# Reciprocals in another step, first keys from float32 rows, half of the first query copies on GpSimd, and the last expert added and stored by 128 tokens

## What is computed

```python
Q, K, V = (heads(x @ W.T + b) for each of q, k, v)      # x is layer-normed first
scores = einsum('bhld,bhrd->bhlr', Q, K) / sqrt(8)
scores = scores + einsum('bhld,lrd->bhlr', Q, rel_k)    # rel_k by clipped distance
attn = softmax(scores)
out = einsum('bhlr,bhrd->bhld', attn, V) + einsum('bhlr,lrd->bhld', attn, rel_v)
x = x + out @ Wo.T + bo
...
# feed-forward: 2 shared experts, 8 routed ones with the best two chosen per token
y = einsum('enh,ehd->end', gelu(einsum('nd,edh->enh', xf, w1) + b1), w2) + b2
x = x + shared_out + einsum('ne,end->nd', comb, y)
```

## Time and profile before

| | |
|---|---|
| median of 3 runs | 2062.05 us (2060.28 to 2062.34) |
| profiled execution: its own time | 2061.96 us |
| profiled execution: span on the chip | 2060.2 us |
| PE busy | 2018.7 us, 98% |
| DVE, ACT, POOL busy | 78%, 73%, 59% |
| granted TensorE clock, mean | 0.995 |

### The profile page before, as it was taken

The page is one execution under the profiler, slowest core; times in us unless marked ns, Lnnn a source line. Parts: engine busy times, 40 slices in busy tenths (PEclk is TensorE's granted clock), DMA queues, the critical chain, the costliest instruction groups (busy, mean ns, idle before and its releaser), DMA issues.

```text
span 2060.2 us, 86849 instructions
## 1 busy us (share of the span) xinstructions
PE 2018.7 (98%) x37410; PEld 1497.1 (73%) x37410; DVE 1606.0 (78%) x3739; ACT 1509.4 (73%) x3341; POOL 1216.6 (59%) x1285
## 2 busy tenths in 40 slices
PE   4999999999999999999999999999999999999999
PEld 3777777777777777777777777777777777777776
DVE  6877897788778877887897788778877777676765
ACT  4767677777677766667667767667666888888887
POOL 4554465456445645554455446445443889988897
PEclk8999999999999999999999999999999999999999
DMA  4212311321231122112211321223122221222120
GB/s 112 74 47 69 83 46 48 83 66 49 57 82 57 47 69 73 55 46 69 77 53 46 84 67 46 57 73 68 46 54 50 27 32 27 28 27 33 24 31 12
DMA packets 256658, 113.05 MB, mean 55 GB/s; under 512 B 143018, under 2 KB 253492, under 8 KB 256276
## 3 DMA queue, kind: packets, MB, share of 16 engines
q1 hardware_dynamic: 255796, 107.10, 21.5%
q10 hardware_dynamic: 480, 0.39, 0.1%
HBM read 83.34 MB, written 8.39 MB: 45 GB/s over the span
## 4 chain that ended last, share of the span: by engine, by line
PE 90%; DVE 5%; ACT 2%; POOL 1%; issue 1%; DMA 0%; SPq 0%; ACTq 0%; DVEq 0%; POOLq 0%
PE ps L1592 21%; PE ps L1527 12%; PE ps L1612 10%; PE ps L1534 9%; PE ps L1622 8%; PE ps L1545 7%; PE ps L1810 3%; PE ps L1812 3%; PE ps L1811 3%; PE ps L1792 3%; PE ps L1794 3%; PE ps L1793 3%; ACT probs L793 1%; DVE keys L1270 1%; PE ps L1501 1%
## 5 line engine op out<-in xcount | busy, mean ns | idle before, releaser
L793 ACT ACTIVATE probs<-ps,neg_max 128x512 f32<-128x512 f32 x1024 | 690.5, 686 | 345.4 <-DVE neg_max L1030 345.3
L1030 DVE TENSOR_REDUCE neg_max<-ps 128x1 f32<-128x512 f32 x1024 | 635.3, 682 | 148.3 <-PE ps L1534 144.3
L557 POOL TENSOR_TENSOR stat_hi<-q_twice,mask8h 128x1024 f16<-128x1024 f16 x128 | 242.5, 1895 | 533.9 <-PE ps L1534 487.9
L1592 PE MATMUL ps<-const,probs 128*128 128x128 f32 x4096 | 500.6, 275 | 4.1 <-issue 1.6
L1592 PEld LDWEIGHTS ps<-const,probs 128*128 128x128 f32 x4096 | 450.2, 141 | 36.1 <-issue 20.3
L1035 DVE COPY probs_t<-ps 128x512 f32<-128x512 f32 x512 | 340.4, 685 | 109.1 <-PE ps L1592 103.7
L783 ACT ACTIVATE probs_t<-ps 128x512 f32<-128x512 f32 x512 | 280.0, 595 | 121.1 <-PE ps L1592 117.1
L690 POOL TENSOR_TENSOR probs_t<-probs,probs_t 128x1024 f16<-128x1024 f32 x160 | 341.4, 2157 | 30.6 <-ACT probs_t L875 29.9
L1527 PE MATMUL ps<-keys,stat_hi 128*32 128x512 f16 x4096 | 318.1, 383 | 0.0
L1534 PE MATMUL ps<-rk_split,stat_rel 96*32 96x512 f16 (+2 forms) x4096 | 281.7, 340 | 0.0
L573 POOL TENSOR_TENSOR stat_rel<-q_rel,mask4h 96x1024 f16<-96x1024 f16 x128 | 251.3, 1963 | 46.2 <-PE ps L1534 30.5
(11 more groups left out here) (192 smaller groups left out, 2861.4 us busy)
## 6 DMA issues: line engine op xcount, KB each, us to landing
rv_step<-in_rv_win SPq DMA_DIRECT2D x128, 512.0 KB, 3.8
keys<-keys SPq DMA_DIRECT2D x56, 96.0 KB, 2.9
x_pair<-in_x SPq DMA_DIRECT2D x8, 512.0 KB, 4.6
rel_scratch<-rel_t SPq DMA_DIRECT2D x256, 16.0 KB, 2.9
x_pair<-in_x SPq DMA_DIRECT2D x16, 256.0 KB, 3.2
x_pair<-rel_scratch SPq DMA_DIRECT2D x64, 64.0 KB, 4.1
out<-keys SPq DMA_DIRECT2D x16, 256.0 KB, 2.3
q_twice<-q_hi SPq DMA_DIRECT2D x28, 128.0 KB, 2.4
```

The lines of the kernel that those rows point to most:

```text
L793: nc.scalar.activation(probs[:, q, :], ps[:, i, :], ACT.Exp, bias=neg_max[:, q:q + 1], accum_out=row_sum[parity][:, s * QUADS + q:s * QUAD ...
L1030: nc.vector.tensor_reduce(neg_max[:, q:q + 1], ps[:, i, :], op=ALU.max, axis=AX_X, negate=True).then_inc(max_done, 1)
L1592: last = nc.tensor.transpose(ps[:, bank, rt * P:(rt + 1) * P], probs[:, q, rt * P:(rt + 1) * P], ident)
```

## The change

It has four parts.

1. The reciprocals of a pair move from round (0, 1) of the next pair to round (7, 1), in the last pair to (4, 1).
2. The first keys: ACT makes a float32 copy `first_wk` of the key weights times the scale, and two float32 copies `first_xn` of the transposed rows out of PSUM. PE projects the first keys with one float32 matmul for each sequence instead of three float16 ones. ACT's copy `first_k` is gone: `k_hi` and `k_lo` are made straight from PSUM.
3. Of the first queries' four copies, the two that stay in their own partitions are made by POOL, as 64x256 float16 copies; SP issues the other two and the two of the low parts. The later columns are still copied by SP alone.
4. The last expert of the last batch writes its four parts of 128 tokens to four banks, with a semaphore for each; DVE adds each part when it is done, and SP stores each with its own DMA.

```diff
+def last_bank(t):
+    return (0, 1, 7, up_bank(EXPERTS - 2, 0))[t]
...
-        first_k = attn_t[:, TOK:2 * TOK].rearrange("p (b c) -> p b c", b=2)
+        first_xn = attn_t[:, TOK:2 * TOK]
...
-                    for copy in range(2):
+                    for copy in range(2) if both else (1 - half,):
                         sp.dma_start(part(q_twice[64 * copy:64 * copy + 64, half, :]), part(q_hi[64 * half:64 * half + 64, :])).then_inc(landed, 16)
...
-            store(B - 1, 1)
-            sp.wait_ge(stored, START + 16 * B)
+            for t in range(TPB):
+                sp.wait_ge(last_ready, t + 1)
+                sp.dma_start(out[(B - 1) * L + t * P:(B - 1) * L + (t + 1) * P, :], acc[:, 1, t, :]).then_inc(last_stored, 16)
+            sp.wait_ge(stored, START + 16 * (B - 1))
+            sp.wait_ge(last_stored, 16 * TPB)
...
             pool.wait_ge(setup_dve, SETUP_FIRST)
+            pool.wait_ge(hi_ready, START + 2)
+            for half in range(2):
+                rows = slice(64 * half, 64 * half + 64)
+                nc.gpsimd.tensor_copy(q_twice[rows, half, :].rearrange("p (b c) -> p b c", b=2)[:, :, 0:P],
+                                      q_hi[rows, :].rearrange("p (b c) -> p b c", b=2)[:, :, 0:P]).then_inc(first_high, 1)
+            pool.wait_ge(first_high, 2)
             for b in range(2):
                 split_low(0, b)
...
-            def first_plain_keys(b, bank):
+            def first_high_keys(b, bank):
                 act.wait_ge(proj_done, START + 2 + b + 1)
-                nc.scalar.activation(first_k[:, b, :], ps[:, bank, :], ACT.Copy, scale=1.0 / W_SCALE).then_inc(k_ready, 1)
-
-            def first_high_keys(b):
-                act.wait_ge(k_ready, START + b + 1)
-                nc.scalar.activation(k_hi[0][:, b, FAR_COLS:KEYS], first_k[:, b, :], ACT.Identity, bias=bks_col[:, 0:1])
-                nc.scalar.activation(k_hi[0][:, b, 0:FAR_COLS], first_k[:, b, FAR * P:L], ACT.Identity, bias=bk_far_col[:, 0:1]).then_inc(hi_ready, 1)
+                nc.scalar.activation(k_hi[0][:, b, FAR_COLS:KEYS], ps[:, bank, :], ACT.Identity, bias=bks_col[:, 0:1]).then_inc(k_ready, 1)
+                nc.scalar.activation(k_hi[0][:, b, 0:FAR_COLS], ps[:, bank, FAR * P:L], ACT.Identity, bias=bk_far_col[:, 0:1]).then_inc(hi_ready, 1)
...
+            nc.scalar.activation(first_wk[:], w_qkv_s[:, 1, :], ACT.Copy, scale=SCALE).then_inc(first_rows, 1)
...
+            for half in range(2):
+                act.wait_ge(xn_low, START + half + 1)
+                nc.scalar.activation(first_xn[:, half * L:(half + 1) * L], ps[:, half, :], ACT.Copy).then_inc(first_rows, 1)
...
-                nc.vector.scalar_tensor_tensor(k_lo[:, b, FAR_COLS:KEYS], first_k[:, b, :], bks_col[:, 0:1], k_hi[0][:, b, FAR_COLS:KEYS], ALU.add, ALU.subtract)
+                nc.vector.scalar_tensor_tensor(k_lo[:, b, FAR_COLS:KEYS], ps[:, bank, :], bks_col[:, 0:1], k_hi[0][:, b, FAR_COLS:KEYS], ALU.add, ALU.subtract)
...
-                if (s, j) == (0, 1) and not first:
+                if (s, j) == (7 if ahead else 4, 1) and not first:
                     reciprocals(pair - 1, 1 - parity)
...
+            def last_expert(b, slot):
+                e = EXPERTS - 1
+                for t in range(TPB):
+                    dve.wait_ge(last_down, t + 1)
+                    nc.vector.scalar_tensor_tensor(acc[:, slot, t, :], ps[:, last_bank(t), 0:D],
+                                                   comb[:, slot, t, e:e + 1], acc[:, slot, t, :], ALU.mult, ALU.add).then_inc(last_ready, 1)
...
             for b in range(2):
-                project_keys(0, b, 2 + b)
+                pe.wait_ge(first_rows, b + 2)
+                nc.tensor.matmul(ps[:, 2 + b, :], first_wk[:], first_xn[:, b * L:(b + 1) * L], start=True, stop=True).then_inc(proj_done, 1)
                 natural_queries(0, b, 6 + b)
```

More of the change, by code:

```diff
@@ L375, in store_rel, with first_queries @@
                     sp.dma_start(rel_scratch[bass.ds(row, 32), cols], rel_t[32 * a:32 * a + 32, twos % 2, :]).then_inc(rel_stored[twos % 2], 16)
[L377 removed]
+            def first_queries(cols, landed, both):
                 def part(rows):
@@ L1321, in batch @@
                 for e in range(EXPERTS):
-                    expert(b, slot, e)
+                    if ahead or e < EXPERTS - 1:
+                        expert(b, slot, e)
+                    else:
+                        last_expert(b, slot)
                     if ahead:
@@ L1812, in down @@
                         last = nc.tensor.matmul(y, hid_l[:, place, k, rows], w2_h[:, e, k, :], start=False, stop=k == 1)
-                last.then_inc(down_done, 1)
+                    if final:
+                        last.then_inc(last_down, 1)
+                if not final:
+                    last.then_inc(down_done, 1)
             def batch(b, slot, ahead, after):
@@ L1823, in batch @@
                         prepare_gates(b + 1, 1 - slot, 1)
-                    down(b, slot, e)
+                    down(b, slot, e, not ahead and e == EXPERTS - 1)
                     if ahead:
```

23 lines of the change are left out of this document (12 added, 11 removed).

## The result

| | |
|---|---|
| before | 2061.76 us, median of 4 (2060.28 to 2062.34) |
| the change | 2072.57 us, median of 4 (2072.21 to 2074.78) |
| ratio | 1.0055, 95% interval 1.0043 to 1.0067 |
| profiled execution: its own time, span | 2072.38 us, 2070.6 us |

The changed kernel is 0.55% slower, where 2056.4 us and faster was predicted.

What follows compares the result with a forecast made beforehand. The prediction took PE as the bound, with 90% of the span, so edits count only where PE stands still. It summed 2061.96 - 4.7 + 0.2 + 0.7 - 1.8 + 0 = 2056.4 us, 8-in-10 range 2054.6 to 2059.6.

Steps and rivals of the forecast that it cites:

- What goes at (1, 0): Without the reciprocals, round (1, 0) falls from 6.95 to 6.28 us in pairs 1 to 7: 4.7 us gained.
- What comes in pairs 1 to 6: Reciprocals at (7, 1) mostly fill DVE's idle time and wait briefly for POOL: 0.2 us lost in all, bounds 0 and 2.1.
- My slower rival: At (7, 1) the third DVE instruction meets stat_rel, PE loses 2.3 us in each of six pairs: 2069.9 us, chance 0.06.
- The sign of being wrong: The forecast would be wrong if the reciprocals' instructions at (7, 1) take over 1 us.
- Pair 7: Reciprocals at (4, 1) meet POOL's stat_rel, maxima begin 1.1 us late: 0.7 us lost once, bounds 0.2 and 1.1.
- Start: Keys 0.3, k_lo 0.86, POOL 0.44 and 0.15: PE's first scores come 1.8 us earlier, bounds 0.8 and 2.8.
- the upper bound of my range for the start: At the start, DVE's head_scaled gets in ahead of stat_hi: 2.8 us gained.
- The float32 matmul: First keys on PE: 512 columns take 0.45 us, against 0.64 for three float16 matmuls, done before ACT comes to it.
- End: Tenth expert's additions begin 0.24 us earlier, but four store DMAs issue later: nothing gained, bounds 0.3 either way.
- The sum: Whole kernel: 2061.96 - 4.7 + 0.2 + 0.7 - 1.8 + 0 = 2056.4 us, own range 2055.2 to 2057.6, chance 0.60.

Runs made afterwards that it cites:

- e4: Changed kernel with the reciprocals at (14, 1), in the last pair at (11, 1) and behind the maxima of (12, 0): 2059.81 us, ratio 0.9993.
- e5: Changed kernel, reciprocals back at (0, 1), one scratch VectorE instruction added per round (s, 1), four forms, four places; trace only: six over 3.7 us, all at (7, 1).
- e7: Changed kernel, reciprocals back at (0, 1), four scratch VectorE instructions at (7, 1), GpSimd's normalisation or waits varied by pair; trace only, control's first scratch instruction 3.84 us.
- e10: Changed kernel with one GpSimd wait for its own last normalisation instruction, ahead of step 9's stat_hi, in pairs 0 to 6: 2057.53 us, ratio 0.9978.
- e13: As e7, with GpSimd's pause at other places of the eight normalisation instructions; trace only: first scratch instruction 3.97 us with six running on, 0.62 with four or fewer.
- e14: As e13, with five tensor_scalar running on, or eight tensor_tensor in place of tensor_scalar; trace only: five shut VectorE out, eight tensor_tensor don't.
- e8: Kernel of e6 with the first queries copied by SP alone, as before the change: first scores at 29.41 us; timed later, 2053.73 us, ratio 0.9964.
- e1: Changed kernel with the reciprocals back at (0, 1), so only the start and end parts are left: 2059.16 us, ratio 0.9988.
- e3: Changed kernel with round (7, 1) done another way in most pairs (instruction form, pieces, earlier place, GpSimd waits); read by trace, no time given.
- e6: Changed kernel, reciprocal at the end of (9, 1), splitting instructions behind (10, 0)'s maxima; last pair (11, 1) and (12, 0): 2055.27 us, ratio 0.9968.

## Why the prediction was wrong

**What goes at (1, 0): right.** Between the same points as in the earlier trace rows, rounds (0, 1) and (1, 0) of pair 1 now take 231.22 to 237.50 and 237.50 to 243.78, 6.28 us each, as forecast. Seven times 0.67 are gained, and the waits went from nine to two.

**What comes in pairs 1 to 6: the failed step.** The prediction let "the next instruction" wait "until POOL's running instruction ends". It waited for four, took 2.90 us, and step 7 grew by 2.69. The term was 0.2 us in all, and it is 6 x 2.69 = 16.1. The sum had no term at all for PE's clock behind such a wait, and that is 1.4 more: 2 x 0.96 - 4 x 0.13. My reading of the rows was right elsewhere in this kernel: e4 and e5 show the wait for one instruction at the other places. It was wrong at (7, 1), because GpSimd comes there from eight tensor_scalar without a pause (shown by e7, e10, e13, e14). The earlier trace rows had a sign that I passed over: there is no idle time ahead of GpSimd's `stat_lo`, and I did not follow its queue back from there to the normalisation. My slower rival (2069.9, chance 0.06) had place, size and nearly the total right, but by another way: it let the third instruction meet `stat_rel`, for which DVE had to be 0.6 us later. The sign of being wrong that I had given, the reciprocals' instructions at (7, 1) "over 1 us", is what happened.

The Trainium skill (SBUF — State Buffer, "Who interferes with whom") says of GpSimd and a VectorE instruction in a two-port mode that whoever issues first gets the shared pair for the whole instruction. Whether ours ran in such a mode no row says, but it waited for GpSimd. e5's other rounds agree with the rule: none over 2.12 us. At (7, 1) the trace differs: `stat_rel`, which began 0.86 us after DVE's instruction had asked, went first. The measurement decides.

**Pair 7: right in kind, 1.0 for 0.7.** The second instruction took 1.31 us (e10's row has the same 1.30), as forecast, and step 4 is 11.93 instead of 10.79 us, 1.14; the next step gives 0.13 back. Of 1.1 us late I had counted 0.4 as hidden, and 0.1 is.

**Start: the size right, one part not.** The first scores moved from 32.09 to 30.40, 1.69 for 1.8 (1.62 from GpSimd's first subtraction on). `k_lo` takes 0.75 and 0.74 beside GpSimd, `q_split` 1.16 both times, `stat_hi` 1.89: as forecast. But part 3, which I took as harmless, costs 1.0 us of a possible 2.7 (e8): without it the upper bound of my range for the start, with `head_scaled` ahead of `stat_hi`, comes true. The float32 matmul was mis-sized, with little effect (ACT stood 0.12 us for the transposes behind the first one): from the second one's start to the next matmul's the timeline has 17.66 to 18.52, 0.86 us, where I had 0.45. The profile has two records for one float32 matmul, and I had taken each for a whole one in the earlier trace rows. The four passes that the Trainium skill (FP8 and Floating Point Precision, "TensorE Precision Notes") gives for true float32 agree with 0.86.

**End: 0 forecast, 0.45 gained.** The four parts were added and stored so:

```profile
2066.75 1.13 DVE L1342 SCALAR_TENSOR_TENSOR keys<-ps,comb,keys 128x128 f32<-128x128 f32 x4
...
2067.13 1.79 SPq L517 DMA_DIRECT2D out<-keys  x4
```

From the start of the ninth expert's additions (2065.59) to the end of the span it is 2070.6 - 2065.59 = 5.01 us, against 2060.2 - 2054.74 = 5.46 in the earlier trace rows. The issues took 0.45 each, as forecast, but 64 KB landed in 1.6 us, not 2.0.

**The sum.** -4.7 + 16.1 + 1.4 + 1.0 - 1.7 - 0.45 = +11.65; the rest of pair 0 is 0.66 shorter (192.12 for 192.78 us from its first maximum to pair 1's, granted clock 0.99 for 0.98). That makes +11.0 of the measured 2072.38 - 2061.96 = 10.4. The 0.66 is chance: this stretch took 192.03 to 194.07 us in kernels that are the same there (the change, e1, e3, e4, e6, e10), so a sum from two profiles is good to a microsecond or two. The last 0.6 is in single steps that differ from run to run: before, 0.86 and 0.28 more in two steps of pairs 3 and 4, after, 0.5 more in one of pair 7.

## What to carry to other kernels

When an instruction of VectorE must pass GpSimd, read the whole run of GpSimd's queue that it lands in, back to the last pause, and not only the instruction that runs. A pause of 0.15 us in the queue that nobody waits for can be worth more than a new place. And read an idle stretch in all repetitions: one pair's trace promised 1.53 us of idle GpSimd at (14, 1), and four of six pairs didn't have it.
